# First attention's scores on 64-row stacks of high and low parts, placed on every fourth partition by DMAs within SBUF

## What is computed

```
x = x + _L0_attn_a_ref(_layernorm(x), W_qkv, W_out)      # causal linear attention, 16 heads of 16
x = x + _L0_ffn_ref(_layernorm(x), W1, b1, W2, b2)       # ternary weights, 256 -> 1024 -> 256
x = x + _L0_attn_b_ref(_layernorm(x), Wq, Wk, Wv, Wo, q_gain, pair_mix)   # window 64, 16 heads, 4 key heads
x = x + _L0_ffn_ref(_layernorm(x), W1, b1, W2, b2)       # the same weights again
```

```
qkv = x @ W_qkv
q, k, v = (to_heads(t) for t in jnp.split(qkv, 3, axis=-1))
phi_q, phi_k = elu(q) + 1.0, elu(k) + 1.0
k_cum = jnp.cumsum(phi_k, axis=2)
kv_cum = jnp.cumsum(jnp.einsum('bhsi,bhsj->bhsij', phi_k, v), axis=2)
numer = jnp.einsum('bhsi,bhsij->bhsj', phi_q, kv_cum)
denom = jnp.einsum('bhsi,bhsi->bhs', phi_q, k_cum) + EPS
attn_out = (numer / denom[..., None]) ... @ W_out
```

## Time and profile before

| | |
|---|---|
| median of 3 runs | 3313.47 us (3312.93 to 3314.41) |
| the profiled execution | 3308.83 us |
| its span, first to last instruction | 3306.9 us |
| TensorE busy | 3088.1 us (93%) |
| VectorE busy | 2398.5 us (73%) |
| ScalarE busy | 1788.9 us (54%) |
| GpSimd busy | 545.9 us (17%) |
| granted TensorE clock, mean | 0.969 |
| mean DMA rate | 14 GB/s |

### The profile page before, as it was taken

How to read it: one execution, slowest core, us unless ns; L and a number is a source line. 1 busy time by engine, 2 the same in 40 slices (tenths; PEclk the granted TensorE clock), 3 DMA queues, 4 the chain that set the end, 5 groups by cost and what they waited for, 6 DMA issues and landing times.

```text
span 3306.9 us, 79649 instructions
## 1 busy us (share of the span) xinstructions
PE 3088.1 (93%) x27330; PEld 2456.8 (74%) x27330; DVE 2398.5 (73%) x5990; ACT 1788.9 (54%) x3585; POOL 545.9 (17%) x1164
## 2 busy tenths in 40 slices
PE   3789999999999999999999999999999999999977
PEld 2567777777777777777777777777777777777755
DVE  4567777777777777777777777777777777777754
ACT  1255555565555565555565555566554556555554
POOL 0012111112111112111112111112111111111111
PEclk9899999999999999999999999999999999999998
DMA  1000000000000000000000000000000000000000
GB/s 60 8 10 16 15 2 15 13 15 15 15 2 15 13 15 15 15 2 15 13 15 15 15 8 9 13 15 15 15 15 2 13 15 15 15 15 2 14 10 16
DMA packets 42084, 44.86 MB, mean 14 GB/s; under 512 B 2608, under 2 KB 41392, under 8 KB 42032
## 3 DMA queue, kind: packets, MB, share of 16 engines
q1 hardware_dynamic: 42032, 44.20, 4.4%
HBM read 21.12 MB, written 16.78 MB: 11 GB/s over the span
## 4 chain that ended last, share of the span: by engine, by line
PE 77%; issue 8%; DVE 6%; ACT 4%; POOL 4%; DMA 0%; POOLq 0%; SPq 0%; DVEq 0%; ACTq 0%
PE Q L364 14%; PE HID L414 13%; PE Y L435 13%; PE Q L555 8%; PE HID L372 4%; PE Q L823 4%; PE Q L593 3%; PE Q L588 3%; PE Q L757 2%; PE Q L606 2%; PE Q L837 2%; PE Q L733 1%; ACT a_qz L1123 1%; PE Q L762 1%; PE Q L570 1%
## 5 line engine op out<-in xcount | busy, mean ns | idle before, releaser
L435 PE MATMUL Y<-w2t,f_hh 128*128 128x256 f32 x2048 | 550.9, 302 | 72.5 <-DVE f_hl L1307 72.3
L949 ACT ACTIVATE f_r<-HID,b1c 128x512 f32<-128x512 f32 x512 | 350.9, 685 | 327.8 <-PE HID L414 240.9
L435 PE MATMUL Y<-w2t,f_hl 128*128 128x256 f32 x2048 | 519.5, 286 | 0.0
L435 PEld LDWEIGHTS Y<-w2t,f_hh 128*128 128x128 f32 x2048 | 395.0, 193 | 141.8 <-DVE f_hl L1307 83.8
L1307 DVE TENSOR_TENSOR f_hl<-f_r,f_hh 128x512 fp32r<-128x512 f32 x512 | 351.6, 687 | 188.1 <-ACT f_hh L950 185.8
L414 PE MATMUL HID<-ff_xh,w1t 128*128 128x512 f32 x1024 | 448.9, 438 | 14.8 <-DVE ff_xl L1299 14.8
L414 PE MATMUL HID<-ff_xl,w1t 128*128 128x512 f32 x1024 | 419.5, 410 | 0.0
L435 PEld LDWEIGHTS Y<-w2t,f_hl 128*128 128x128 f32 x2048 | 397.1, 194 | 4.2
L1409 DVE TENSOR_TENSOR a_s<-Q,cst 128x512 f32<-128x512 f32 x512 | 329.3, 685 | 76.6 <-PE Q L555 68.9
L950 ACT ACTIVATE f_hh<-HID,b1c 128x512 fp32r<-128x512 f32 x512 | 351.9, 687 | 0.0
L1123 ACT ACTIVATE a_qz<-Q 128x512 f32<-128x512 f32 x512 | 279.1, 602 | 46.8 <-PE Q L762 46.5
(11 more groups left out here) (186 smaller groups left out, 7048.4 us busy)
## 6 DMA issues: line engine op xcount, KB each, us to landing
x<-in_x SPq DMA_DIRECT2D x32, 512.0 KB, 4.2
out<-x SPq DMA_DIRECT2D x32, 512.0 KB, 3.0
b_vm<-b_v SPq DMA_DIRECT2D x64, 96.0 KB, 2.1
a_s<-in_w SPq DMA_DIRECT2D x1, 1024.0 KB, 8.0
a_qz<-in_w SPq DMA_DIRECT2D x1, 1024.0 KB, 10.2
a_s<-in_w_qkv SPq DMA_DIRECT2D x1, 768.0 KB, 4.7
cst<-in_const SPq DMA_DIRECT2D x1, 389.0 KB, 5.6
a_qT<-in_w_b SPq DMA_DIRECT2D x1, 384.0 KB, 5.9
```

The lines of the kernel that those rows point to most:

```text
L435: mm = pe.matmul(Y[t // 2][:, (t % 2) * D:(t % 2 + 1) * D], h[:, fb % 2, t * P:(t + 1) * P], w2t[:, fb, :], start=False, stop=(fb == FB - ...
L949: act.activation(f_r[:, fb % 2, :], HID[fb % 2][:], ACT.Relu, bias=b1c[:, fb:fb + 1]).then_inc(f_rr, 1)
```

## The change

Each fp32 phi is split into a float32r high part and a float32r low part: ScalarE copies the high one (`split_hi`), VectorE subtracts (`split_lo`). The parts go to `a_khl` (on `a_s[:, 0]`) and `a_qhl` (on `a_qz`). The SP queue then copies them within SBUF into stacks: of the 32 rows of a head pair (`2 * HD`), each row stands on four neighbouring partitions of the stack, for keys (high, low, high, low), for queries (high, high, low, low). One DMA moves one term of one group of 32 partitions of one half `k`: it reads 32 neighbouring partitions and writes every fourth partition of the stack (`row:P:4`). The keys need 4 terms x 4 groups x 2 halves = 32 DMAs of 32 rows by 512 columns (2 KB a row, 64 KB in all), the queries twice as many of 256 columns (1 KB a row, 32 KB), in two batches of 32: first the columns of chunks 0 and 1, then those of 2 and 3. Key stacks lie in `b_qs` and a new buffer `a_ks`, query stacks in `b_qT`. A matmul on 64 rows then covers one head of 16 dims with all four products, so that no zeroed copies of the queries are wanted and `by_parity` goes. `scores(ch, pair)` issues 8 float32r matmuls on 64 rows, 128 columns wide. Its first call waits for the 32 DMAs of the keys and the first 32 of the queries, `scores(2, 0)` for the last 32.

```diff
+        a_khl = a_s[:, 0].rearrange("p (t k) n -> p t k n", t=2).bitcast(F32R)
+        a_qhl = a_qz[:, :].bitcast(F32R)
+        a_qs = b_qT[:, :].rearrange("p g b n -> p (g b n)").rearrange("p (t n) -> p t n", t=2 * REP)
+        a_ks = (b_qs[:, :].rearrange("p u h s d -> p (u h s d)").rearrange("p (t n) -> p t n", t=REP),
+                sb("a_ks", [P, REP, S], F32R)[:, :])
...
+            def stack(dst, src, terms, cols, done):
+
+                for row, term in enumerate(terms):
+                    for g in range(REP):
+                        for k in range(KB):
+                            sp.dma_start(dst[k][row:P:4, g, cols].bitcast(F32), src[2 * HD * g:2 * HD * (g + 1), term, k, cols].bitcast(F32)).then_inc(done, 16)
+
+            def stack_keys(a):
+
+                sp.wait_ge(a_kq_lo, a * 4 + 2)
+                stack(a_ks, a_khl, (0, 1, 0, 1), slice(0, S), a_kst)
+
+            def stack_queries(a):
+                sp.wait_ge(a_kq_lo, a * 4 + 4)
+                for half in range(2):
+                    stack((a_qs[:, 0:REP], a_qs[:, REP:]), a_qhl, (0, 0, 1, 1), slice(half * S // 2, (half + 1) * S // 2), a_qst[half])
+
             def phase1(s):
                 if s.last:
                     store(s.c)
+                if s.a is not None:
+                    stack_keys(s.a)
+                    stack_queries(s.a)
...
                     def scores(ch, pair):
 
                         if ch == 0 and pair == 0:
-                            pe.wait_ge(a_qz_s, (a + 1) * 4)
-                            pe.wait_ge(a_ph, (a + 1) * 4)
-                        else:
+                            pe.wait_ge(a_kst, (a + 1) * 512)
+                        if ch % 2 == 0 and pair == 0:
+                            pe.wait_ge(a_qst[ch // 2], (a + 1) * 512)
+                        if ch or pair:
 
                             pe.wait_ge(a_sm, a * 16 + 4 * ch + 2 * pair)
                         for k in range(KB):
-                            for n in range(2):
-                                r = 2 * pair + n
-                                rows = slice(32 * r, 32 * r + 32)
-                                mm = pe.matmul(Q[n][:, k * 2 * P:(k + 1) * 2 * P].rearrange("p (e q) -> p e q", e=2),
-                                               a_kT[rows, k, ch * P:(ch + 1) * P], a_qz[rows, k, :, ch * P:(ch + 1) * P],
-                                               start=(k == 0), stop=(k == KB - 1), skip_group_check=True)
-                                if k == KB - 1:
-
-                                    mm.then_inc(a_sc[n], 1)
+                            for i in range(2):
+                                for e in range(2):
+                                    g, rows, at_col = k * REP + 2 * pair + i, slice(64 * e, 64 * e + 64), (2 * k + i) * P
+                                    mm = pe.matmul(Q[e][:, at_col:at_col + P], a_ks[k][rows, 2 * pair + i, ch * P:(ch + 1) * P],
+                                                   a_qs[rows, g, ch * P:(ch + 1) * P],
+                                                   start=(k == 0 and i == 0), stop=True, skip_group_check=True)
+                                    if k == KB - 1 and i:
+
+                                        mm.then_inc(a_sc[e], 1)
...
+                    def split_hi(j):
+                        act.wait_ge(a_ph, a * 4 + j + 1)
+                        if j < 2:
+                            if s.b is not None and needed(s.b * NT):
+
+                                act.wait_ge(b_lo, s.b * NT)
+                            act.activation(a_khl[:, 0, j, :], a_kT[:, j, :], ACT.Copy).then_inc(a_kq_hi, 1)
+                        else:
+                            if s.b is not None and needed(s.b * NT):
+
+                                act.wait_ge(b_o, s.b * NBL * KVH)
+                            act.activation(a_qhl[:, 0, j - 2, :], a_qT[:, j - 2, :], ACT.Copy).then_inc(a_kq_hi, 1)
+
...
-                    def by_parity(m):
-
-                        dve.wait_ge(a_ph, a * 4 + 2 + m + 1)
-                        for e in range(2):
-                            dve.tensor_scalar(a_qz[:, m, e, :], a_qT[:, m, :], C["parity"][:, e:e + 1], None,
-                                              ALU.mult).then_inc(a_qz_s, 1)
+                    def split_lo(j):
+                        dve.wait_ge(a_kq_hi, a * 4 + j + 1)
+                        src, dst = ((a_kT, a_khl), (a_qT, a_qhl))[j // 2]
+                        dve.tensor_tensor(dst[:, 1, j % 2, :], src[:, j % 2, :], dst[:, 0, j % 2, :],
+                                          ALU.subtract).then_inc(a_kq_lo, 1)
```

More of the change, by code:

```diff
@@ L50 @@
 SAFE_SCORE = 40.0
-_WIDTHS = dict(ident=P, causal=P, heads=HB * HV, parity=2, qodd=P, qfirst=P,
+_WIDTHS = dict(ident=P, causal=P, heads=HB * HV, qodd=P, qfirst=P,
                cos=NT * HD, sin=NT * HD)
@@ L682, in phase1 @@
                     project(3)
+                    down(3)
                     qkv(s.b, 1, a + 1)
@@ L685, in phase1 @@
                     qkv(s.b, 3, a + 1)
-                    down(3)
                 def phase2(s):
@@ L729, in turn_qk @@
                             pe.wait_ge(f_act, (carry + 1) * FB)
+                        if t == 3 and j == 0:
+                            pe.wait_ge(b_te, b * 12 + 9)
                         src = b_ks[:, t % 2] if j == 2 else b_qs[:, t % 2, 8 * j:8 * j + 8]
@@ L874, in phase2 @@
                     numer(0)
+                    scores(2)
                     numer(1)
-                    scores(2)
                     up(0)
+                    up(1)
                     turn_numer(0)
-                    up(1)
                     scores(3)
+                    turn_qk(2, 0)
                     numer(2)
+                    turn_y(0)
+                    turn_qk(2, 1)
+                    turn_qk(2, 2)
                     down(0)
-                    turn_y(0)
-                    turn_qk(2, 0)
-                    turn_qk(2, 1)
+                    project(0)
                     numer(3)
-                    turn_qk(2, 2)
-                    project(0)
-                    down(1)
+                    up(2)
                     scores(4)
@@ L892, in phase2 @@
                     turn_qk(3, 0)
-                    up(2)
+                    down(1)
+                    numer(4)
                     turn_y(1)
-                    numer(4)
                     scores(5)
-                    project(1)
                     turn_qk(3, 1)
                     turn_qk(3, 2)
+                    project(1)
                     numer(5)
@@ L902, in phase2 @@
                     scores(6)
+                    turn_numer(2)
                     up(3)
                     next_norm(1)
-                    turn_numer(2)
+                    turn_y(2)
+                    down(2)
+                    scores(7)
                     numer(6)
-                    down(2)
-                    turn_y(2)
-                    scores(7)
-                    up(4)
                     project(2)
@@ L914, in phase2 @@
                     turn_numer(3)
-                    down(3)
+                    up(4)
                     turn_y(3)
@@ L1049, in phase1 @@
                     qk_exp(0)
+                    qk_exp(1)
+                    split_hi(0)
+                    split_hi(1)
+                    qk_exp(2)
                     relu(5)
-                    qk_exp(1)
-                    qk_exp(2)
+                    split_hi(2)
+                    qk_exp(3)
+                    split_hi(3)
+                    relu(6)
                     values(0)
-                    values(1)
-                    relu(6)
-                    qk_exp(3)
                     relu(7)
                     keys(0)
+                    own_norm()
+                    values(1)
                     keys(1)
-                    own_norm()
                     relu(0)
@@ L1175, in phase2 @@
                     y_hi(1)
-                    relu(2)
                     exps(5)
@@ L1184, in phase2 @@
                     y_hi(2)
+                    relu(3)
                     exps(7)
-                    relu(3)
                     evacuate_numer(3)
+                    y_hi(3)
                     relu(4)
-                    y_hi(3)
                 norm_hi(at, 0, Q)
@@ L1496, in phase1 @@
                     mask(3, (2, 3))
+                    low(2)
                     y_lo(2)
+                    next_norm_lo(1)
+                    f1_stats(0)
+                    residual(2)
                     f1_stats(1)
-                    next_norm_lo(1)
-                    residual(2)
-                    low(2)
                     normalise(3)
```

205 lines of the change are left out of this document (106 added, 99 removed).

## The result

| | before | after |
|---|---|---|
| median | 3313.2 us (3311.26 to 3314.41, 4 runs) | 4578.07 us (4573.04 to 4585.26, 4 runs) |
| span of the profiled execution | 3306.9 us | 4579.6 us |
| granted TensorE clock, mean | 0.969 | 0.829 |

The ratio is 1.382, 95% interval 1.380 to 1.384: the kernel is 38% slower, 39.5 us a step over 32 steps. The forecast was 4372 us, its range 3900 to 4740. The direction and the mechanism were right; the time is that of the rival in which every issue takes 0.64 us (4585). The kernel before and the kernel after are called "before" and "after" from here on.

What follows compares the result with a forecast made beforehand. TensorE, busy 93%, was taken to bound the kernel. Per step 31.5 us of later scores, less 0.4 for matmuls, plus 2 of clock, made 33.1; over 32 steps 1059 us, hence 4372 us, range 3900 to 4740.

Steps and rivals of the forecast that it cites:

- the rival in which every issue takes 0.64 us: SP's queue: every issue behind a copy within SBUF takes 0.64 us whatever its rows; 39.7 us a step, 4585 us, chance 25%.
- What bounds, and where the change bites: TensorE, busy 93%, bounds the step with nearly no slack; it would wait at the first scores and at chunk 2.
- The distance of two issues: Spacing of the 96 stack DMAs a step on SP's queue, taken as 0.57 us, bounds 0.44 and 0.64.
- c: The distance of two DMA issues on SP, 0.57 us; 95 of them stand before the last stack DMA.
- When the stacks begin: SP's first stack DMA, waiting for the low parts of both key halves: T + 2.7, allowed T + 2 to T + 3.5.
- T: Start of up(5), the first unit of phase 1; before, chunk 2's scores start at T + 27.55, forecast T + 59.0.
- landing: Time from a stack DMA's issue to its data being there: 2.1 us, overlapping the next issues.
- The matmuls: New score calls on TensorE: 0.1 us gained a call, four calls counting, 0.4 us a step, at most 2.
- The clock: TensorE's clock falls behind the waits; slow work behind scores(2, 0) costs 2 us a step, range nothing to 6.
- "The same set" of units ahead of `scores(2, 0)`: TensorE's units ahead of and behind scores(2, 0) are the same set in both kernels; the new order was costed at nothing.
- the rival of cheap issues: SP issues at 0.2 us or less, so the cover holds and the matmul gain shows: about 3270 us, chance 3%.
- ScalarE and VectorE, costed at nothing: Splits add 2.4 us on ScalarE and 2.7 on VectorE a step; both have room, 1 to 2 us without cover.

Runs made afterwards that it cites:

- the merged form: After, with one DMA for both halves k: queries only (64 DMAs a step) 3945.95 us; keys and queries (32 a step) 3650.41 us.
- the run with the old scores: After's order on every engine with the fp32 scores and by_parity of before, no splits or stacks: 3620.47 us, ratio 1.091.
- the run without stacks: After with stacks written for the first sequence only, later scores on stale data, splits and order kept: 3531.1 us, ratio 1.064.
- the new matmuls alone: Before with only the score calls of sequences 2 and on replaced by the new ones, on stale tiles, no stacks: 3215.09 us, ratio 0.970.
- the two reordered attempts: After's order with up(0), up(1) between state calls and VectorE work moved: stacks for first sequence only, ratio 1.081; 32 merged DMAs, ratio 1.103.
- the run with the state calls: Before with the three state calls of the first attention in a row ahead of the first scores: 3411.07 us, ratio 1.030.
- the merged run: After with one DMA for both halves k of keys and queries, all 512 query columns at once, 32 DMAs a step: 3650.41 us, ratio 1.101.

## Why the prediction came out as it did

**What bounds, and where the change bites: right.** The step has no slack, TensorE waits at exactly the two places named, the first scores and those of chunk 2, in all 32 sequences, and nothing behind the waiting matmul fills it. The forecast was 24 us at the first and a few at the second; the rows say 22.75 and 7.96. TensorE's share, near 70%, is 71%.

**The distance of two issues: mis-sized, 0.57 for 0.636.** The term of the sum that was off is c, and the step of the argument that failed is "a stack DMA has 32 rows where `b_vm` has 64, so of the 0.13 that the second copy takes more than the first I count half". The rows of a DMA play no part: a stack DMA takes the 0.59 us of the second `b_vm` copy with half its rows. Its bytes play next to none: the distance is 0.635 at 32 KB, 0.636 at 64 KB, 0.65 to 0.66 at 64 and 128 KB in the merged form. What does play a part stood in the rows of before: the first copy within SBUF of a run is short (0.51 here), and each DMA behind such a copy takes 0.59 to 0.60 and a gap, as the second `b_vm` copy and the load behind it did; the setup loads, with no copy within SBUF ahead, are 0.51 us apart. In the form with both halves `k` even the first takes 0.61 us. Why, no run here shows. The Trainium skill (DMA: Bandwidth & Descriptors, the table of sequencer cycles) would give an estimate of 0.43 from its 512 cycles for the generations before the newest; the measured distance, 0.64, decides, and is further from it than my own value was.

I had the 0.64 as an upper bound and gave it 25%; it was also the row nearest in kind.

**When the stacks begin: 1 us late.** It is T + 3.7 in place of T + 2.7, outside the 2 to 3.5 that I allowed. I counted one phi behind ScalarE's last relu; VectorE did both key halves there, 1.29 us for 0.69, which is 0.6 of the 1.0:

```profile
1561.28 1.29 DVE L1438 SCALAR_TENSOR_TENSOR a_kT<-a_eq,a_relu 128x512 f32<-128x512 f32 x2 [0.45 <-ACT a_relu L1055]
```

With landing 1.9 for 2.1 the sum is 3.7 + 95 x 0.636 + 1.9 = 66.0, and the row says T + 66.1.

**The matmuls: mis-sized, 0.1 for 0.47 a call.** Of my two rows, transposes with 128 weight columns and the second attention's 64-row call, I took the wrong one. A new call takes 0.59 us at full clock (1616.39 to the next unit at 1616.98), the old one 1.06. "The number of weight loads is what stays" did not decide.

**The clock: 2 us taken, some 2.4 in the common step (an estimate, 0.5 + 1.9), 5.1 in the one shown first.** All are in the 0 to 6 allowed. In the common step the part behind `scores(2, 0)` grew by 0.5 us, in the other by 2.8, where the two terms of the sum gave 2 - 0.4 = 1.6.

**How the errors add up.** The forecast was 33.1 us a step and the result 39.5, so 6.4 are missing. The distance gives 95 x 0.066 = 6.3 of them, the later start 1.0, the landing -0.2. That leaves some -0.7 for the matmuls and the clock together, an estimate over all steps: the matmuls' -1.5 is partly made up by the clock. So the distance is as large as the whole miss by luck, since the other three errors cancel.

**"The same set" of units ahead of `scores(2, 0)`, costed at nothing: wrong in itself, without effect on the sum.** This is the reading that failed without showing in the time. The order costs 9.6 us a step when nothing covers it (the run with the old scores). In after it lies ahead of `scores(2, 0)` and inside the waits: TensorE reached its first scores at T + 23 and not at T + 16.8, and the stacks were there 22.75 us later still. Had the issues been cheap, the rival of cheap issues, 3270 us, would have come out near 3531, the run without stacks, and not faster at all. So the 3% for faster was too much, for a reason I had not seen.

**ScalarE and VectorE, costed at nothing: close, and not measured apart.** With the full splits ScalarE's values are late by up to 3.5 us, 27.8 us in total, under 1 us a step and inside the wait. Without the splits, in the new order, TensorE waits for the values 9.8 us in total and 0.7 at most; so some 18 us in total are the splits' doing. The times agree: the run without stacks is 89 us quicker than the one with the old scores, and the new matmuls alone give 99, which leaves some 10 us for the splits, no more than those runs spread.

## What stays open

Of the order's 9.6 us a step the three state calls in a row are 3.1. Which move costs the rest was not settled: at that place TensorE's work comes in small pieces with gaps and the clock falls, but no run moved the other units one by one, and the two reordered attempts brought waits of their own. That the clock falls because of the gaps is suggested by the stretches of the kernels with the new order and shown by none; the run with the state calls shows that 1.2 us of gaps a step alone do not do it. Nor does TensorE's busy time in a few us settle it. Two stretches of the second phase, first in before and then in the run with the state calls, columns as in the earlier trace rows:

```profile
1467.07:1471.07 4.00, 3.14 (x19) 2.60 (x18) 2.96 (x11) 1.27 (x2) 3.56 (x8) 1.00 0.21 49
1471.07:1475.07 4.00, 2.67 (x15) 2.27 (x16) 3.79 (x12) 2.58 (x5) 0.27 (x1) 0.87 0.00 0
```

```profile
1414.40:1418.40 4.00, 3.14 (x19) 2.60 (x18) 2.96 (x11) 1.26 (x2) 3.56 (x8) 1.00 0.21 49
1418.40:1422.40 4.00, 2.67 (x18) 2.24 (x18) 3.79 (x12) 2.58 (x5) 0.28 (x1) 1.00 0.00 0
```

TensorE is busy 3.14 and 2.67 of 4 us in both, and the clock falls in the first (to 0.50 in the 4 us behind) and stays whole in the second. So the clock also falls in the kernel before, at another place, and what decides it is open.

## What to carry to other kernels

Count the issues of a DMA queue and multiply by the spacing of two that follow each other, not by the length of a lone one: a layout change by 96 small DMAs is 61 us of queue, however few its bytes. Merge them over a free dimension first, then use a second queue, then give the trick only to the part of the work that lies late enough to hide it. Here the half that is hidden, with merged DMAs, two queues and the order of before, wins 2.0%; the whole loses 38% with 96 DMAs and 10% with 32. And price a new order by itself before a large wait hides it, since two costs in the same place show as one.

## What the runs showed of the hardware

- The distance of DMAs within SBUF on SP's queue is 0.635 to 0.66 us for 32, 64 and 128 KB, with 32 rows read and every fourth partition written (after, the merged run).
- GpSimd's queue issues them 0.55 us apart, its engine being busy for all of it; they landed in 2.0 us (64 KB) and in 3.7 us (128 KB) by the median. On SP's queue the landing was 2.1 and 2.6 us.
- Eight float32r matmuls of 64 rows by 128 columns take 0.59 us at full clock, eight fp32 passes of 32 rows by 256 columns 1.06.
- TensorE's clock went from 1.00 to 0.50 for 10 us behind a stretch in which it was busy 3.37 us of 5, without any long wait, and stayed at 1.00 in another kernel behind 3.14 and 2.67 us of 4.
